# Scatter groups held back by one block in a four-layer graph kernel

## The reference

```python
# layer 0: a dense bias, the weight of edge (dst, src) in its cell, the last of equal edges wins
bias = jnp.full((n, n), NEG, dtype=x.dtype)
bias = bias.at[diag, diag].set(0.0)
bias = bias.at[dst, src].set(edge_weight.astype(x.dtype))
qkv = x @ Wqkv.T + bqkv
scores = jnp.einsum('hnd,hmd->hnm', q, k) / np.sqrt(HEAD_DIM) + bias[None, :, :]
attn = jax.nn.softmax(scores, axis=-1)
# layers 1 to 3: sums over edges, all of which can be written with counts of edges
# between each pair of nodes, for each of four edge types
agg = jax.ops.segment_sum(msg, dst, num_segments=n)
```

## Time and profile before

| | us |
|---|---|
| median of 3 runs | 628.55 |
| lowest and highest run | 623.87, 629.28 |
| the profiled execution | 631.25 |
| its span, first to last instruction | 629.5 |

### The profile page before, as it was taken

How to read it: one execution, slowest core, us unless ns; L and a number is a source line. 1 busy time by engine, 2 the same in 40 slices (tenths; PEclk the granted TensorE clock), 3 DMA queues, 4 the chain that set the end, 5 groups by cost and what they waited for, 6 DMA issues and landing times.

```text
span 629.5 us, 7530 instructions
## 1 busy us (share of the span) xinstructions
PE 563.1 (89%) x2433; PEld 355.0 (56%) x2448; DVE 384.2 (61%) x939; ACT 242.9 (39%) x510; POOL 238.4 (38%) x210
## 2 busy tenths in 40 slices
PE   6998999993988999987999899996999998999691
PEld 2443444462843446666767688864877784445560
DVE  7986988993069868967646413134245416884736
ACT  3100700062247864573642221213433116885434
POOL 6565666668554004307213152333152664000000
PEclk8999999997999999997999899997999998999986
DMA  8720000022556000247222142244251844000001
GB/s 275 315 71 2 0 0 0 0 69 79 186 154 180 4 2 0 68 106 179 75 76 86 48 133 68 67 134 125 77 183 52 247 128 126 0 1 2 1 1 67
DMA packets 29383, 53.32 MB, mean 85 GB/s; under 512 B 4945, under 2 KB 6429, under 8 KB 28838
## 3 DMA queue, kind: packets, MB, share of 16 engines
q1 hardware_dynamic: 15436, 26.09, 14.0%
q0 software_dynamic: 11968, 19.96, 11.0%
q10 hardware_dynamic: 1946, 6.85, 3.3%
HBM read 50.73 MB, written 2.17 MB: 84 GB/s over the span
## 4 chain that ended last, share of the span: by engine, by line
PE 67%; DVE 17%; ACT 6%; issue 5%; POOL 2%; DMA 2%; ACTq 0%; DVEq 0%; POOLq 0%
PE bank L478 18%; PE bank L455 11%; PE bank L456 11%; PE bank L457 11%; PE bank L568 4%; PE bank L545 3%; PE bank L552 3%; DVE h L1040 2%; DVE sp L1193 2%; PE bank L447 2%; POOL edge_bias L364 1%; ACT waste L762 1%; ACT gap L762 1%; DVE h L1049 1%; DVE h L1048 1%
## 5 line engine op out<-in xcount | busy, mean ns | idle before, releaser
L341 POOL TENSOR_TENSOR wl<-wraw,wh 128x512 fp32r<-128x512 f32 (+1 forms) x82 | 106.9, 1324 | 98.7 <-DMA wh<-w 33.1
L478 PE MATMUL bank<-hot 128*128 128x512 bf16 x529 | 118.9, 383 | 5.6 <-DVE hot L1097 4.8
L478 PEld LDWEIGHTS bank<-hot 128*128 128x128 bf16 x544 | 53.4, 99 | 70.8 <-DVE hot L1097 6.2
L364 POOL DMA_INDIRECT edge_bias<-ewn,cell_at x68 | 76.5, 1125 | 44.3 <-DVE cell_at L1091 19.1
L455 PE MATMUL bank<-th,wl 128*128 128x512 f32 x104 | 43.4, 417 | 15.0 <-POOL wl L341 12.4
L455 PE MATMUL bank<-wh,tl 128*128 128x512 f32 x112 | 46.2, 412 | 3.0 <-DVE tl L1008 3.0
L457 PE MATMUL bank<-wh,th 128*128 128x512 f32 x112 | 44.4, 397 | 0.0
L456 PE MATMUL bank<-wl,th 128*128 128x512 f32 x112 | 44.4, 397 | 0.0
L456 PE MATMUL bank<-tl,wh 128*128 128x512 f32 x104 | 42.8, 411 | 0.0
L457 PE MATMUL bank<-th,wh 128*128 128x512 f32 x104 | 42.3, 407 | 0.0
L777 ACT ACTIVATE sp<-sp,peak 128x512 f32<-128x512 f32 x44 | 31.7, 720 | 25.7 <-DVE peak L1193 25.4
(11 more groups left out here) (194 smaller groups left out, 1083.2 us busy)
## 6 DMA issues: line engine op xcount, KB each, us to landing
wraw<-w SPq DMA_DIRECT2D x26, 256.0 KB, 2.9
wh<-w POOLq DMA_DIRECT2D x6, 1024.0 KB, 5.8
keyb<-edge_keys ACTq DMA_DIRECT2D x4, 1088.0 KB, 12.0
wh<-w_rel POOLq DMA_DIRECT2D x4, 1024.0 KB, 5.8
wraw<-w_rel SPq DMA_DIRECT2D x16, 256.0 KB, 2.7
wraw<-w_qkv SPq DMA_DIRECT2D x12, 256.0 KB, 6.4
wraw<-w_o SPq DMA_DIRECT2D x8, 256.0 KB, 3.0
wh<-w_o POOLq DMA_DIRECT2D x2, 1024.0 KB, 5.8
```

What stands on the lines that cost most here:

```text
L341: pool.tensor_tensor(wl[n % WSLOTS][:, k, 0:width], wraw[:, q % 3, 0:width], wh[n % WSLOTS][:, k, 0:width], ALU.subtract).then_inc(s["w_lo ...
L364: pool.indirect_dma_start(out=bias_dram, out_offset=bass.IndirectOffsetOnAxis(ap=cell_at[:, c:c + 1], axis=0), in_=ewn[:, c:c + 1], in_off ...
L478: mm = pe.matmul(ps(name)[:], hot[:, slot, 0, i * P:(i + 1) * P], hot[:, slot, 1 + kind, :], start=False, stop=last, skip_group_check=True)
```

## The change

One wait is added on POOL, ahead of the first scatter of each of the groups 0 to 13. `hot_ready` counts chunks of one-hots written, so `(g + 4) * 4` is reached when block g+3 is complete. Before, group g could start when it was settled, right after block g+2 was complete. For groups 14 to 16 no such wait is made (there is no block 17 and beyond).

```diff
@@ -359,6 +359,8 @@
             for c in range(CHUNKS):
                 if c % GROUP == 0:
                     pool.wait_ge(s["placed"], c // GROUP + 1)
+                    if c // GROUP + FIRST_PLACED + 2 <= TBLOCKS:
+                        pool.wait_ge(s["hot_ready"], (c // GROUP + FIRST_PLACED + 2) * RING)
                 if c >= WINDOW:
                     pool.wait_ge(scattered[c % WINDOW], 16 * (c // WINDOW))
                 pool.indirect_dma_start(out=bias_dram, out_offset=bass.IndirectOffsetOnAxis(ap=cell_at[:, c:c + 1], axis=0),
```

## The result

| | before | after |
|---|---|---|
| median of the runs, us | 627.16 (7 runs, 623.83 to 629.51) | 632.06 (7 runs, 630.83 to 638.07) |
| profiled execution, us | 631.25 | 631.98 |
| span, us | 629.5 | 630.2 |

The ratio is 1.0095, 95% interval 1.0049 to 1.0142. The forecast of +3.0 us is a ratio of 1.005. The two profiled executions differ by 0.7 us only, and the reason for that is part of the reading.

What follows compares the result with a forecast made beforehand. First stage: PE's sweeps bound it to about 123 us, then POOL's last scatters and `low(1)`, for which PE waits. The gap's -2.0 and the tail's +5.0 gave +3.0 us, 631.6 us, range 627.0 to 636.0.

Steps and rivals of the forecast that it cites:

- The gap, -2.0: Sweep 1: breaking up the queue of 13 scatters removes PE's 2.02 us gap, blamed on a late report to DVE.
- The rival that took the stall to be larger in the usual run: Sweep 1: removing the stall gives 5 us and pays back the loss, sum 0, 628.6 us; chance 12%.
- The tail, +5.0: End of POOL's queue: 16 scatters instead of 12 ahead of `low(1)`, four more at 1.28 us, landing on PE.
- the rival of the dear tail: End of the queue: added scatters at 1.80 us beside unpacking, 7.2 instead of 5.0, slower by over 1%; chance 15%.
- The added waits, sweep 2: 0: Sweep 2: each block still sees one group, PE has no gap to give back; worth 0.
- Behind the end: After the scatters: weight and bias loads and products shift as a block; PE's lower clock costs 1.8 us before and after alike.
- The sum: Whole kernel: -2.0 + 5.0 = +3.0 us, 631.6 us on the median of 628.55.
- Within 1%: Whole kernel: a change under 1% (6.3 us) either way, given 0.80.
- The lock's rule: Tail: a DVE instruction on the shared port locks GpSimd out, so scatters behind DVE's last run free, 5.1 not 7.2.

Runs made afterwards that it cites:

- ctl: The kernel before, measured again with no edit: 629.88 against 628.66 us, ratio 1.002.
- hold_last: The kernel before with one wait only, group 13 waiting for the one-hots of block 16: 633.06 against 628.66 us, ratio 1.010.
- hold_early: The kernel before with the whole block's wait for groups 0 to 3 only: 627.63 against 626.70 us, ratio 1.0009.
- fade: The kernel before with waits for groups 0 to 8 that shrink from a whole block to nothing: 626.92 against 628.66 us, ratio 0.9987.
- after2: The changed kernel measured a second time with no edit: 631.80 against 629.77 us, ratio 1.0018.
- pile: The kernel before with one wait, group 4 waiting for the one-hots of block 9, so scatters queue up in sweep 2: 645.02 against 628.66 us, ratio 1.0277.
- no_early: The kernel before with the 16 scatters of groups 0 to 3 left out (result wrong): 628.36 us in one run.
- k_early: The kernel before with `low(1)` (k's weight) moved forward on POOL, ahead of the scatters of groups 15 and 16: 624.52 against 626.70 us, ratio 0.9956.
- k_early_fade: k_early plus the shrinking waits of fade: ratio 0.9972 to the kernel before.
- after_k_early: The changed kernel, all fourteen waits, with `low(1)` moved forward as in k_early: ratio 1.0045 to the kernel before.
- kv_early: k_early with two pieces of `low(2)` (v's weight) also moved forward, between group 16's scatters: 624.48 against 629.77 us, ratio 0.9893 to the kernel before.
- kv_early_fade: kv_early plus the shrinking waits of fade: 623.75 us, ratio 0.9892 to the kernel before.

## Why the prediction was right

Taken by its own steps. In the table, the start of sweep 2 is the first matmul of line 478 (480 and so on in the edited kernels) behind the bank setting; the tail is the end of the last scatter less the end of sweep 2.

| profiled execution of | sweep 2 starts, us | tail, us | attention starts, us | from there to the end, us |
|---|---|---|---|---|
| before | 69.62 | 16.7 | 178.4 | 451.1 |
| ctl | 72.08 | 16.1 | 180.0 | 448.2 |
| hold_last | 67.85 | 20.6 | 181.7 | 446.4 |
| hold_early | 67.08 | 16.1 | 175.0 | 450.5 |
| fade | 67.24 | 16.1 | 176.6 | 448.5 |
| after | 67.72 | 21.2 | 181.5 | 448.8 |
| after2 | 67.45 | 21.8 | 181.6 | 451.0 |
| pile | 67.40 | 16.1 | 193.0 | 451.0 |
| no_early | 67.03 | 17.8 | 178.0 | 448.6 |
| k_early | 68.38 | moved | 175.6 | 447.0 |
| k_early_fade | 67.35 | moved | 174.2 | 448.3 |
| after_k_early | 67.47 | moved | 176.5 | 450.1 |
| kv_early | 68.12 | moved | 172.9 | 448.0 |
| kv_early_fade | 67.36 | moved | 172.4 | 448.1 |

("Moved": other work of POOL stands between the scatters, so this column does not apply.)

**The gap, -2.0.** Right in mechanism and in this pair of executions (1.9 us). As the value of the term it is one draw. Six profiled kernels issue their scatters in sweep 1 as the kernel before does (before, ctl, hold_last, k_early, kv_early, pile); their sweep 2 starts at 69.62, 72.08, 67.85, 68.38, 68.12 and 67.40 us, 68.9 on average. The seven that hold groups back (after, after2, fade, hold_early, after_k_early, k_early_fade, kv_early_fade) lie between 67.08 and 67.72, 67.4 on average. The change takes away 1.5 us on average, and between 0 and 4.7 in one execution. The prediction took the gap of one execution for a fixed part of the kernel before; in truth its size is drawn anew in each execution. The rival that took the stall to be larger in the usual run has no support, either: on the average of these six it is a little smaller. A small misreading: the queue of 13 scatters begins at 36.97 us; from 38.34 on it has 12.

**The tail, +5.0.** Right. Four tails without the wait on group 13 (before, ctl, hold_early, fade) average 16.25 us, three with it 21.2: +5.0. With `pile` and `no_early` the six without average 16.5, and it is +4.8. In the first pair alone it is +4.5, and PE's wait grew by 4.6 us (10.7 to 15.3). From the end of sweep 2 to the attention it takes 51.4 to 51.9 us in the three kernels with the wait and 45.6 to 48.6 in the six without, so the whole amount does land on PE. All four added scatters came at 1.28 us, and none at 1.80, so the rival of the dear tail did not happen. The tail's sixteen scatters beside waiting engines brought no late report with them.

**The added waits, sweep 2: 0.** Right: 62.32 us in both.

**Behind the end.** The forecast that k's product, v's and the attention shift as a block held: +2.66 at k, +3.0 at the attention. The lower clock behind PE's restart was not quite alike: from 158 to 162 us the granted clock was 0.94 before and 0.52 after, though PE restarted only 2.66 us later. That the rest of the program is the same from one execution to the next did not hold. From the attention's start to the end it takes 446.4 to 451.1 us in kernels that are identical there. That is why the profiled execution of after was 631.98 and not 634.3 us, and why the profiles alone would say +0.7.

**The sum.** +5.0 less 1.5 is +3.5 us, 0.6%. The first measurement gives +3.1 to +8.9 us by its interval, the second -0.8 to +3.0; the sum lies inside the first and just above the second. "Within 1%" was right for both. The median of after, 632.06, is 0.5 us from the 631.6 forecast, and some of that closeness is luck: the forecast stood on a median of 628.55 us from three runs, seven runs gave 627.16, and the change between the medians is +4.9 us the first time and +2.0 the second, on either side of the +3.0 forecast.

**The lock's rule.** The sentence of the Trainium skill (SBUF — State Buffer, the section on the two separate sides) that gave 5.1 and not 7.2 for scatters behind DVE's last instruction agrees with the rows of 145.16 to 150.30. For the late reports in `pile` it gives no answer: during its wait of 11.87 us DVE had no instruction running, and the scatters beside it took 0.98 us each, as they do alone.

**Left open.** Why PE's reports come late beside some queues of scatters and not beside others. In `hold_early` 20 scatters in a row did no harm, in `pile` a queue of 24 stopped DVE for 11.87 us. That the reports are held until the queue ends is seen in the semaphore's times; what holds them is not. No run here changed the way in which PE's reports reach DVE. Open as well is why the two measurements of the same pair differ (1.0095 and 1.0018), and where after_k_early loses what its profile does not show.

## What to carry to other kernels

Before work is held back to spread it out, look at the end of the queue that it stands in: what is postponed by one period there is paid in full when something on the path waits behind the queue, here 5.0 us for four scatters ahead of one weight (`hold_last`). Hold back early and let the delay shrink to nothing before the end (`fade`), or better, take out of the queue's shadow what the next stage needs (`kv_early`, 1.1% faster), and count all that hangs on it: the first attempt moved one weight and met the next. A gain read from one execution's stall is a draw and needs a second profile before it enters a sum.

## What the runs showed of the hardware

With indirect DMAs issued from POOL at a pitch of 1.28 us, a report from PE to DVE can come very late: DVE's waits were up to 4.3 us in the kernel before and 11.87 us in `pile`, and the longest ended 2 us after the last scatter of the queue. The semaphore was raised up to 19.7 us after PE had ended the chunk (90.01 and 109.72 in `pile`), and the increments held back came within 0.3 us of each other in the kernel before (55.85 to 56.12). Where four scatters at a time are followed by a rest of about 1.4 us or more, no wait was over 0.9 us (after, 46 to 122 us).

Left to itself, the same code of 448 us takes up to 4.7 us more or less, with PE's granted clock at its lower level at different places: near 349 and 527 us in the first execution of before and not in that of after, near 264 us the other way round. For a question of 0.5% a pair of profiles is not enough.
